# An eight-layer kernel on one core: the third layer's closing steps done chunk by chunk inside its scan

## What is computed

```python
q = silu(x @ wq); k = x @ wk; v = x @ wv             # 16 heads of 8
z = cumlogsumexp([0, k]); log_f = z[:-1] - z[1:]; k = exp(k - z[1:])
q = [q*cos, q*sin]; k = [k*cos, k*sin]               # 16 features per head
def step(S, (qt, kt, vt, lt)):                       # over 2048 tokens
    S = exp(lt) * S + kt * vt ;  o = q . S
g = o * sigmoid(x @ wg1 @ wg2)
normed = g / sqrt(mean over the head of g*g + 1e-6) * norm_w
return normed @ wo
```

## Time and profile before

| | before |
|---|---|
| median of 3 runs (lowest, highest) | 1189.37 us (1188.11, 1190.2) |
| profiled execution, its own time | 1189.36 us |
| its span, first to last instruction | 1187.6 us |
| mean granted TensorE clock | 0.930 |
| VectorE / TensorE / ScalarE / GpSimd busy, share of the span | 72% / 81% / 55% / 54% |

### The profile page before, as it was taken

How to read it: one execution, slowest core, us unless ns; L and a number is a source line. 1 busy time by engine, 2 the same in 40 slices (tenths; PEclk the granted TensorE clock), 3 DMA queues, 4 the chain that set the end, 5 groups by cost and what they waited for, 6 DMA issues and landing times.

```text
span 1187.6 us, 11501 instructions
## 1 busy us (share of the span) xinstructions
PE 963.5 (81%) x3005; PEld 552.3 (47%) x3005; DVE 850.0 (72%) x1146; ACT 653.4 (55%) x1187; POOL 639.1 (54%) x448
## 2 busy tenths in 40 slices
PE   6779875888779863799999999875878777774996
PEld 3334332333247432688888888431323323233784
DVE  5995348999676476566666666588999898735664
ACT  5855776000444751455655555778657575362555
POOL 3030134999410141577777777305989898632672
PEclk9979997999999976899999999987989898988998
DMA  2000300000110000766667676000000000001651
GB/s 76 1 0 1 117 16 1 0 1 0 35 27 1 17 7 18 162 148 146 154 140 161 137 159 150 2 0 1 0 0 1 0 1 0 0 20 40 153 135 36
DMA packets 18645, 61.29 MB, mean 52 GB/s; under 512 B 2560, under 2 KB 12416, under 8 KB 12800
## 3 DMA queue, kind: packets, MB, share of 16 engines
q1 hardware_dynamic: 18608, 60.86, 21.8%
HBM read 59.15 MB, written 1.70 MB: 51 GB/s over the span
## 4 chain that ended last, share of the span: by engine, by line
PE 40%; DVE 18%; POOL 10%; issue 7%; ACT 5%; DMA 2%; POOLq 0%; SPq 0%; DVEq 0%; ACTq 0%
PE ps L407 39%; POOL g L1512 6%; DVE g L1540 3%; DVE g L1842 2%; DVE y L2093 2%; ACT rstd L962 2%; ACT g L962 2%; DVE resid L1540 2%; DVE g L2049 1%; POOL rstd L1521 1%; DVE tmp L1540 1%; DMA g<-coef_scratch 1%; DVE parts L1540 1%; DVE g L2093 1%; POOL g L1499 1%
## 5 line engine op out<-in xcount | busy, mean ns | idle before, releaser
L407 PE MATMUL ps<-parts 128*128 128x512 f32 x1704 | 411.8, 402 | 31.4 <-DVE g L1540 12.2
L407 PEld LDWEIGHTS ps<-parts 128*128 128x128 f32 x1704 | 324.5, 192 | 118.0 <-DVE g L1540 13.0
L1463 POOL TENSOR_TENSOR parts<-g,parts 128x512 fp32r<-128x512 f32 x168 | 217.5, 1295 | 156.2 <-ACT parts L962 152.2
L962 ACT ACTIVATE g<-ps 128x512 f32<-128x512 f32 (+2 forms) x298 | 175.9, 595 | 197.1 <-PE ps L407 168.0
L407 PE MATMUL ps<-g,arena 128*128 128x512 f32 (+1 forms) x392 | 191.2, 627 | 38.5 <-POOL g L1499 18.4
L1540 DVE TENSOR_TENSOR ps<-g,ps 128x512 f32<-128x512 f32 x168 | 116.9, 696 | 109.4 <-PE ps L407 87.6
L1512 POOL TENSOR_TENSOR g<-g 128x1024 f32<-128x1024 f32 x64 | 149.0, 2359 | 50.7 <-DVE g L1540 50.7
L962 ACT ACTIVATE parts<-g 128x512 fp32r<-128x512 f32 (+2 forms) x252 | 126.3, 534 | 35.3 <-DVE g L1540 18.0
L1540 DVE TENSOR_TENSOR g<-ps,g 128x512 f32<-128x512 f32 (+1 forms) x164 | 115.5, 704 | 39.6 <-DMA g<-coef_scratch 16.1
L407 PEld LDWEIGHTS ps<-g,arena 128*128 128x128 f32 (+1 forms) x392 | 74.5, 197 | 148.4 <-issue 85.2
L962 ACT ACTIVATE sq<-ps 128x512 f32<-128x512 f32 x56 | 33.1, 596 | 146.5 <-PE ps L407 144.5
(11 more groups left out here) (180 smaller groups left out, 1094.1 us busy)
## 6 DMA issues: line engine op xcount, KB each, us to landing
g<-coef_scratch SPq DMA_DIRECT2D x80, 512.0 KB, 6.2
g<-in_moe_dram SPq DMA_DIRECT2D x42, 192.0 KB, 4.7
g<-in_rope_dram SPq DMA_DIRECT2D x1, 2048.0 KB, 8.7
arena<-in_weights_dram SPq DMA_DIRECT2D x1, 1348.5 KB, 5.8
arena<-in_weights_dram SPq DMA_DIRECT2D x1, 1028.5 KB, 4.9
g<-in_x_dram SPq DMA_DIRECT2D x4, 256.0 KB, 3.9
out_dram<-g SPq DMA_DIRECT2D x4, 256.0 KB, 2.5
arena<-in_weights_dram SPq DMA_DIRECT2D x1, 838.0 KB, 7.1
```

The lines of the kernel that those rows point to most:

```text
L407: return nc.tensor.matmul(o, lhsT, rhs, start=start, stop=stop, **kw)
L962: return nc.scalar.activation(o, i, func, **kw)
L1463: pv.tensor_tensor(hid_lo[:, cols(c)], g[:, 6, (c % 2) * N:(c % 2 + 1) * N], hid_hi[:, cols(c)].bitcast(F32), ALU.subtract).then_inc(s["hl ...
```

## The change

The tail of layer 2 is done chunk by chunk. The tail of chunk c - 1 is placed in each engine's list between the scan steps of chunk c; the tail of chunk 3 stays behind the scan.
- VectorE: `gated_heads(c-1)` after step (c, 1), `normed_heads(c-1)` after (c, 3), `tail_add(c-1)` (the two instructions `tmp` and `resid`) after (c, 6), `tail_h(c-2)` after (c, 0) for c >= 2. Behind the scan: `tail_h(2)`, `gated_heads(3)`, the sign matrices, then `normed_heads(3)`, `tail_add(3)`, `tail_h(3)`.
- TensorE: `tail_var(0..2, c-1)` and `tail_out(c-1)` ahead of `sum_heads` of steps (c, 1), (c, 3), (c, 4) and (c, 6).
- ScalarE: squares (now also those of `resid` for the next norm, which GpSimd did) and the logs and exponentials, between the copies of v.
- The banks of sums are a ring of two (0 and 3), which the three variances of the chunk use too, those of the decays a ring of two (1 and 2), and the output matmul has bank 4. ScalarE writes the decays of chunk c + 1 during chunk c instead of all three ahead of the scan.
- Some semaphores that are used once are merged into counted ones; names move, waits stay where they were.

The diff, cut to the layer concerned (the renamed semaphores are left out):

```diff
@@ -44,7 +44,7 @@
 LAYERS = 8
 
 
-NORMS = ["pre0", "ln1", "ln2", "rms", "post2", "pre3", "post3",
+NORMS = ["pre0", "ln1", "ln2", "post3",
          "pre4", "post4", "pre5", "post5", "pre6", "post6", "pre7", "post7"]
 NORM = {name: i for i, name in enumerate(NORMS)}
 
@@ -57,14 +57,17 @@
          ("pre", 1, 2), ("pre", 2, 0), ("post", 0, 3), ("pre", 1, 3), ("post", 1, 1), ("pre", 2, 1),
          ("post", 1, 2), ("pre", 2, 2), ("post", 1, 3), ("pre", 2, 3)]
 SETUP = {name: i + 1 for order in (("bias_bank", "nam_wc_bank", "nam_bias_bank", "wo_bank", "wg_bank", "mo_bank"),
-                                   ("bias_ready", "nam_wc", "nam_bias", "mo_ready"),
-                                   ("nam_setup", "wo_read", "setup2", "f_setup")) for i, name in enumerate(order)}
+                                   ("decay_ready", "mixed_ready", "bias_ready", "nam_wc", "nam_bias", "mo_ready"),
+                                   ("zeroed", "rest_ready", "decay_negated", "nam_setup", "wo_read", "setup2", "f_setup")) for i, name in enumerate(order)}
 FR_BANKS = (0, 1, 2, 5)
 FK_BANKS = (4, 3)
 FV_BANK, NAM_S_BANK, CENTRE_BANK = 0, 1, 7
 ROOT_BANKS = (5, 6)
 NAM_BANKS = (2, 3, 4, 0)
 Q_BANKS = (7, 1)
+HEAD_BANKS = (0, 3)
+DECAY_BANKS = (1, 2)
+WO_BANK = 4
 BIG = 1e30
 B_BANK, C_BANK = 4, 5
 DA_BANKS = (2, 6)
...
@@ -254,7 +256,10 @@
             return sq[:, k // 4 % 2 * N:(k // 4 % 2 + 1) * N]
 
         def fast_decay(c):
-            return ps[:, 1 + c, :]
+            return ps[:, DECAY_BANKS[c % 2], :]
+
+        def heads(c):
+            return ps[:, HEAD_BANKS[c % 2], :]
 
         def v_bank(k):
             return 5 + k % 3
...
@@ -699,24 +704,45 @@
                 e, c = k % 8, k // 8
                 if k == 0:
                     pe.wait_ge(s["gate_ready"], CHUNKS)
+                if c >= 2 and e == 0:
+                    pe.wait_ge(s["root_ready"], len(ROOTS) + 3 * (c - 1))
                 pe.wait_ge(s["qm_ready"], k + 1)
                 for r in range(2):
-                    last = mm(ps[:, c, :], W(2, "head_sum", e * 128, e * 128 + 128),
+                    last = mm(heads(c), W(2, "head_sum", e * 128, e * 128 + 128),
                               g[:, 2, (2 * (e % 2) + r) * N:(2 * (e % 2) + r + 1) * N],
                               e == 0 and r == 0, e == 7 and r == 1)
                 last.then_inc(s["qm_used"], 1)
 
+            def tail_var(which, matrix, c):
+                pe.wait_ge(s["tail_square"], 3 * c + which + 1)
+                mm(heads(c), matrix, tmp[:, cols(c)]).then_inc(s["root_bank"], 1)
+
+            def tail_out(c):
+
+                pe.wait_ge(s["nrm_ready"], c + 1)
+                if c:
+                    pe.wait_ge(s["x_ready"], x_at(3) + c)
+                mm(ps[:, WO_BANK, :], wo_normed, y[:, cols(c)]).then_inc(s["centred"], 1)
+
             for k in range(8 * CHUNKS):
+                e, c = k % 8, k // 8
                 if k + 3 < 8 * CHUNKS:
                     spread_v(k + 3)
+                if c and e == 2:
+                    tail_var(0, W(2, "head_mean"), c - 1)
+                if c and e == 4:
+                    tail_out(c - 1)
+                if c and e == 5:
+                    tail_var(1, averaging, c - 1)
+                if c and e == 7:
+                    tail_var(2, averaging, c - 1)
                 if k:
                     sum_heads(k - 1)
             sum_heads(8 * CHUNKS - 1)
-            variance("rms", 0, W(2, "head_mean"))
-            for c in range(CHUNKS):
-                pe.wait_ge(s["nrm_ready"], c + 1)
-                mm(ps[:, c, :], wo_normed, G(5, c)).then_inc(s["centred"], 1)
-            boundary(2)
+            tail_var(0, W(2, "head_mean"), CHUNKS - 1)
+            tail_out(CHUNKS - 1)
+            tail_var(1, averaging, CHUNKS - 1)
+            tail_var(2, averaging, CHUNKS - 1)
 
 
             pe.wait_ge(s["setup_done"], SETUP["f_setup"])
...
@@ -1187,17 +1213,55 @@
                 f(G(12, c), ps[:, NAM_BANKS[c], :], ACT.Sigmoid).then_inc(s["gate_ready"], 1)
             use_log_exp()
             act.wait_ge(s["gate_ready"], CHUNKS)
-            for c in range(1, CHUNKS):
+
+            def decay(c):
+
                 act.wait_ge(s["kr_ready"], c + 1)
+                if c >= 2:
+                    act.wait_ge(s["st_ready"], 8 * (c - 1))
                 f(fast_decay(c), G(4, c), ACT.Identity, scale=-1.0, bias=one).then_inc(s["decay2_ready"], 1)
-            for k in range(3, 8 * CHUNKS, 4):
+
+            def copy_v(k):
                 act.wait_ge(s["vb_bank"], k + 1)
                 if of_pool(k) > 2:
                     act.wait_ge(s["in_pool"], of_pool(k) - 2)
                 f(v_copy(k), ps[:, v_bank(k), :], ACT.Copy).then_inc(s["v_copied"], 1)
-            square("rms", lambda c: G(4, c), "og_ready", 0)
-            rstd_of("rms", eps6, 0)
-            boundary(2)
+
+            def rms_square(c):
+                act.wait_ge(s["og_ready"], c + 1)
+                f(tmp[:, cols(c)], G(4, c), ACT.Square).then_inc(s["tail_square"], 1)
+
+            def post_square(c):
+                act.wait_ge(s["centred"], CHUNKS * 3 + c + 1)
+                f(tmp[:, cols(c)], ps[:, WO_BANK, :], ACT.Square).then_inc(s["tail_square"], 1)
+
+            def pre_square(c):
+                act.wait_ge(s["x_ready"], x_at(3) + c + 1)
+                f(tmp[:, cols(c)], resid[:, cols(c)], ACT.Square).then_inc(s["tail_square"], 1)
+
+            def tail_root(n, eps):
+
+                c = n // 3
+                act.wait_ge(s["root_bank"], len(ROOTS) + n + 1)
+                chain(f(rstd[:, cols(c)], heads(c), ACT.Ln, bias=eps))
+                chain.wait()
+                f(rstd[:, cols(c)], rstd[:, cols(c)], ACT.Exp, scale=-0.5).then_inc(s["root_ready"], 1)
+
+            for c in range(CHUNKS + 1):
+                if c < CHUNKS:
+                    copy_v(8 * c + 3)
+                if c + 1 < CHUNKS:
+                    decay(c + 1)
+                if c:
+                    rms_square(c - 1)
+                    tail_root(3 * c - 3, eps6)
+                if c < CHUNKS:
+                    copy_v(8 * c + 7)
+                if c:
+                    post_square(c - 1)
+                    tail_root(3 * c - 2, eps5)
+                    pre_square(c - 1)
+                    tail_root(3 * c - 1, eps5)
 
 
             act.wait_ge(s["setup_done"], SETUP["f_setup"])
@@ -1475,7 +1539,7 @@
                 round_of(r0 + pairs, 1, False)
 
             for layer in range(2, LAYERS):
-                if layer > 2:
+                if layer > 3:
                     square(f"pre{layer}", R, "x_ready", x_at(layer))
                 if layer == 5:
                     experts(5, 32, 0, 0)
...
@@ -1823,6 +1887,24 @@
                 tt(two_of(0, 11, k), g[:, 6:8, cols(k // 8)],
                    ps[:, v_bank(k):v_bank(k) + 1, :].to_broadcast([P, 2, N])).then_inc(s["vb_used"], 1)
 
+            def gated_heads(c):
+                dve.wait_ge(s["qm_used"], 8 * c + 8)
+                tt(G(4, c), G(12, c), heads(c)).then_inc(s["og_ready"], 1)
+
+            def normed_heads(c):
+                dve.wait_ge(s["root_ready"], len(ROOTS) + 3 * c + 1)
+                tt(y[:, cols(c)], G(4, c), rstd[:, cols(c)]).then_inc(s["nrm_ready"], 1)
+
+            def tail_add(c):
+                dve.wait_ge(s["root_ready"], len(ROOTS) + 3 * c + 2)
+                chain(tt(tmp[:, cols(c)], ps[:, WO_BANK, :], rstd[:, cols(c)]))
+                chain.wait()
+                tt(R(c), R(c), tmp[:, cols(c)], ALU.add).then_inc(s["x_ready"], 1)
+
+            def tail_h(c):
+                dve.wait_ge(s["root_ready"], len(ROOTS) + 3 * c + 3)
+                tt(H(c), R(c), rstd[:, cols(c)]).then_inc(s["h_ready"], 1)
+
             inputs(0)
             for k in range(8 * CHUNKS):
                 if k + 1 < 8 * CHUNKS and (k + 1) % 4 != 3:
@@ -1842,10 +1924,16 @@
                     last = v.tensor_tensor_scan(state, fast_decay(c), two_of(0, 11, k)[:, r, :],
                                                 state[:, N - 1:N] if c else 0.0, ALU.mult, ALU.add)
                 last.then_inc(s["st_ready"], 1)
-            for c in range(CHUNKS):
-                dve.wait_ge(s["qm_used"], 8 * c + 8)
-                tt(G(4, c), G(12, c), ps[:, c, :]).then_inc(s["og_ready"], 1)
-            scale_by_rstd("rms", lambda c: G(5, c), lambda c: G(4, c), "nrm_ready")
+                if c and e == 0 and c >= 2:
+                    tail_h(c - 2)
+                if c and e == 1:
+                    gated_heads(c - 1)
+                if c and e == 3:
+                    normed_heads(c - 1)
+                if c and e == 6:
+                    tail_add(c - 1)
+            tail_h(CHUNKS - 2)
+            gated_heads(CHUNKS - 1)
 
             dve.wait_ge(s["w_loaded"], 64)
             dve.wait_ge(s["bools_loaded"], 16)
@@ -1855,7 +1943,10 @@
             v.tensor_scalar(scales[:, 0:1], W(3, "s", 0, 1), 4.0, None, ALU.mult)
```

(19 more changed lines are left out.)

37 lines of the change are left out of this document (12 added, 25 removed).

## The result

The changed kernel takes 1194.28 us (median of 20 runs, 1190.56 to 1196.86), the kernel before 1190.16 (20 runs, 1186.91 to 1193.22). The ratio is 1.0033, with a 95% interval of 1.0022 to 1.0044: 3.9 us more, between 2.6 and 5.2. The prediction was 1193.0, +3.6.

What follows compares the result with a forecast made beforehand. VectorE was taken to bound the scan, and a chain of short hand-overs the tail. Scan +10.3, new tail 23.4, old tail -30.0 gave +3.6 us on 1189.36: 1193.0 us, range 1188.3 to 1197.5.

Steps and rivals of the forecast that it cites:

- part 1: Scan of layer 2: 14 instructions added to VectorE, which has no idle time, lengthen it by 10.3 us.
- The upper bound of 12: Scan: the most it lengthens, in us, if each of eight two-buffer instructions waits 0.5 or so.
- the stated range: Whole kernel: 1188.3 to 1197.5 us.
- Who comes first: Scan, `H` and scaled heads: VectorE starts ahead of GpSimd, so these five cost about 0.61 us each, 3.1 together.
- part 2: Scan: waits inserted in the engines' lists stall nothing, with slacks of 2.4, 1.5 and over 3 us.
- The rival of the late root: Scan: at the lower clock `tmp` stalls 1.4 us in each of three chunks, +4.2, 1197.2 us; chance 0.10.
- part 3: Tail behind the scan, chunk 3 only: 23.4 us up to layer 3, bounds 20.2 and 24.6, against 30.0 before.
- The chain of 20.2: Tail: links from the scan's end to layer 3, in us, before the clock's cost is added.
- three of four matmuls at the lower level: Tail: three of the later four single matmuls run at TensorE's 1.2 GHz, adding 2.4 us.
- the late last product, 0.8: Tail: GpSimd's last product waits about 0.8 us for sum (3, 5), which stands behind a 2.6 us pause.
- The rival with the clock up: Tail and scan: upper clock holds through the chain and `resid` finds the pair free, 1187.6 to 1188.4 us; chance 0.20.

Runs made afterwards that it cites:

- load: Kernel before plus 14 unneeded VectorE products of the change's kinds and places, tail untouched: 1197.07 us, ratio 1.0061 to the kernel before.
- lock: Changed kernel with `tmp` and `resid` moved behind step (c, 7), `H` behind the gate product of (c, 1): 1201.90 us, ratio 1.0092 to the kernel before.
- narrow: Changed kernel with its 14 moved VectorE products 8 columns wide instead of 512, waits kept: 1188.65 us, ratio 0.9987 to the kernel before.
- filled: Changed kernel plus 11 spare matmuls in TensorE's pauses around and behind the last sums: 1190.87 us, ratio 1.0006 to the kernel before.
- mix_filled: `mix` plus six spare matmuls around the last variance: 1188.12 us, ratio 0.9973 to the kernel before.
- mix: Changed kernel with only gate products and scaled heads kept in the scan, the rest behind it, reordered: 1186.96 us, ratio 0.9971 to the kernel before.
- wave: Kernel before with its tail, wholly behind the scan, staggered chunk by chunk: 1190.60 us, ratio 1.0000 to the kernel before.
- wave_gates: `wave` with gate products, squares and first variances of chunks 0 to 2 back in the scan: 1187.70 us, ratio 0.9975 to the kernel before.

## Why the prediction was right

- **The scan, 10.3 us longer** (part 1): measured 10.16. `resid` 1.08 each (1.1 taken), `tmp` 0.70 (0.72), heads and `H` 0.58 (0.61), which make 3.2 + 2.1 + 2.9; the gate products are the rest, 1.9 (1.8). `load` showed that the instructions alone do it, `lock` that the price holds for these places only, and `narrow` that GpSimd's product sets the end of `resid`: of the 1.16 us at 254.85, 0.60 are waiting (until 255.45). The upper bound of 12 in part 1 was added wrongly (8.8 + 8 x 0.5 = 12.8); the stated range holds the time that it gives.
- **Who comes first**: VectorE, in all five, as forecast from 0.15 us between the two starts. GpSimd's product beside them is 2.72; 2.9 was said, since I took the whole of VectorE's instruction, and it had a start of 0.15.
- **No inserted wait stalls** (part 2): no idle VectorE in the scan, clock 0.97. The rival of the late root is out. That the slacks were real is seen in `lock`, where `resid` ended 4.7 us later behind its step (c, 6) than here; that was more than the slack of over 3 us ahead of the third variance, and VectorE had to wait.
- **The tail, 23.4** (part 3): measured 22.84. The chain of 20.2 was right (20.24 in `filled`), and so were three of four matmuls at the lower level (0.69 + 0.94 + 0.94 = 2.6; 2.4 taken). The term that was wrong is the late last product, 0.8. The sum at 313.86 stood behind a pause of 2.63 us, as that of the earlier trace rows had, but took 1.98 us for its four records and not 3.57, so the product at 316.80 wasn't late (at 3.57 us it would have been, by 0.85). I took one row's clock for a rule about a pause of that length, and it isn't one (last section). The 0.2 us missing on the other side are in the lower level's price.
- **The rival with the clock up** was given 0.20 for the case that both its terms hold. `filled` shows its tail of 20.2 exists, but only with spare matmuls.
- **The sum**: +3.6 predicted, +3.0 in the two stretches, +3.9 (2.6 to 5.2) in the medians. The 0.9 between the last two is within the measurement. Layer 2's end was put at 316.2 and the first matmul of layer 3 at 339.6; 316.72 and 339.56 were measured, both with a scan that began 0.6 us later. That the second fits to 0.04 is luck: the late beginning made up for a tail 0.6 shorter than forecast. That the median fits to 0.3 is luck too, since 0.9 of it lies outside the two stretches that were summed.
- What I hadn't priced: the last product, 2.6 us late before, comes in time in `load`, which shortens the old tail by 2.4. It takes both a scan that is slow enough and the sum's upper level: in `narrow`, with a scan 4.4 us longer than before's, the product was 1.1 late. The lateness was in the 30.0 of the old tail, so the sum holds it, but I had put its end down to the new order of the tail. Of the 7.2 us by which the tail shrank, 2.4 come with the slower scan and 4.8 from the new order.

## What to carry to other kernels

Work that was moved beside the full engine cost its whole time there (10.1 us for 14 products); only a chain of hand-overs was saved. So move the short steps that start the chain (here gates and heads, 0.6 us each) and leave the ones that come with a wait (`resid`, 1.08) where the engine has time. A VectorE product of two buffer operands waited for the GpSimd product that was running, however narrow it was: place it right behind the instruction whose end also releases GpSimd. Single matmuls with pauses between them can fall to the lower clock (three of four here, 2.6 us); count that in, or fill the pauses with spare matmuls and measure whether it reaches the time (it did in `filled`, not in `mix_filled`).

## What the runs showed of the hardware

- A product of 128 x 8 took 1.15 us beside a GpSimd product, and 0.13 to 0.14 elsewhere. The 128 x 512 ones that waited ended 0.54 to 0.56 us after GpSimd's (`resid` at 254.85, 1.16; in `lock` at 291.87, 2.35; in `mix` at 309.64, 2.13), the narrow one 0.01 after it. Where another GpSimd product stood behind (253.10, 5.12 for two), it ran after VectorE's.
- Three of the four late matmuls of the tail ran at the lower level, after pauses of 2.17, 0.69 and 3.55 us, but not the first, after 1.44. In `narrow` the one behind the same 2.17 ran at the upper level (320.69, 1.13 us). With spare matmuls in the pauses (`filled`) all four ran at the upper level.
- A sum behind a pause on TensorE ahead of the scan's last steps ran at the lower level after 2.62 us in the kernel before, 2.44 in `narrow` and 2.62 in `wave`, and at the upper level after 2.63 in the changed kernel, 2.64 in its repetition, 2.62 in `load`, 2.63 in `lock` and 2.62 in `wave_gates`. So the length of the pause doesn't decide it. What does was not tried and stays open.
